# Cross-attention and FFN layer on one core: two of k's four feature chunks turned by DMA as fp16 parts, c turned scaled and split

## The reference

```
q = softmax over each head's 64 features of (Wq @ layernorm(x)), 8 heads, times 64**-0.5
k = softmax over the 1024 tokens of (Wk @ c);   v = Wv @ c
context = k v^T per head;  out = Wo @ (context^T q) + bo
x = x + out / |out| * g * sqrt(128)                      # norm over the 128 channels
x = x + layernorm(x) @ dequantised 4-bit weight + bias   # FFN, 1024 x 1024
```

## Time and profile before

| | us |
|---|---|
| median of 3 runs | 719.55 (717.13 to 721.21) |
| profiled execution | 717.66 |
| its span | 715.8 |
| PE busy | 655.5 (92%) |
| DVE busy | 547.5 (76%) |
| POOL busy | 482.8 (67%) |
| ACT busy | 448.4 (63%) |

### The profile page before, as it was taken

How to read it: one execution, slowest core, us unless ns; L and a number is a source line. 1 busy time by engine, 2 the same in 40 slices (tenths; PEclk the granted TensorE clock), 3 DMA queues, 4 the chain that set the end, 5 groups by cost and what they waited for, 6 DMA issues and landing times.

```text
span 715.8 us, 11150 instructions
## 1 busy us (share of the span) xinstructions
PE 655.5 (92%) x3320; PEld 419.8 (59%) x3320; DVE 547.5 (76%) x890; ACT 448.4 (63%) x743; POOL 482.8 (67%) x413
## 2 busy tenths in 40 slices
PE   4878699999999999999999999999999999999655
PEld 3645466666665666666665666666565666666232
DVE  3996897887888887887888887887888887886421
ACT  3666758566675848576775748576775748575411
POOL 3156484968768594958778594958778594957541
PEclk9979999999999999999999999999999999999977
DMA  8135135573735445463625445463726444453602
GB/s 294 60 59 134 43 79 130 100 164 89 163 59 161 89 111 129 98 161 88 172 48 164 85 114 128 95 161 88 175 45 170 79 109 79 91 104 88 119 29 59
DMA packets 180983, 78.95 MB, mean 110 GB/s; under 512 B 170440, under 2 KB 172000, under 8 KB 180960
## 3 DMA queue, kind: packets, MB, share of 16 engines
q1 hardware_dynamic: 174624, 55.61, 37.1%
q10 hardware_dynamic: 6336, 23.07, 9.5%
HBM read 28.32 MB, written 8.39 MB: 51 GB/s over the span
## 4 chain that ended last, share of the span: by engine, by line
PE 35%; POOL 25%; issue 19%; DVE 12%; ACT 6%; DMA 2%; SPq 1%; POOLq 0%; ACTq 0%; DVEq 0%
PE ps_m L1093 7%; POOL q_tok_lo L409 6%; PE ps_m L1032 3%; POOL x L474 3%; POOL q_exp L399 3%; POOL y L415 3%; DVE q_sum L773 3%; POOL c_lo L439 3%; PE ps_k L962 3%; POOL rn L458 2%; PE ps_k L964 2%; PE ps_k L963 2%; ACT k_exp L522 2%; DVE q_nmax L761 2%; PE ps_o L962 2%
## 5 line engine op out<-in xcount | busy, mean ns | idle before, releaser
L409 POOL TENSOR_TENSOR q_tok_lo<-q_exp,q_tok_hi 128x1024 f16<-128x1024 f32 x64 | 139.3, 2176 | 87.3 <-ACT q_tok_hi L538 87.3
L399 POOL TENSOR_TENSOR q_exp<-q_exp,q_rec 128x1024 f32<-128x1024 f32 x64 | 122.1, 1908 | 5.0
L1032 PE MATMUL ps_m<-k_t,c_t 128*128 128x512 f32 x256 | 120.0, 603 | 0.0
L527 ACT ACTIVATE q_exp<-q_exp 128x512 f32<-128x512 f32 x128 | 80.6, 630 | 44.3 <-DVE q_exp L766 44.2
L754 DVE TENSOR_REDUCE k_nmax<-ps_k 128x1 f32<-128x1024 f32 x64 | 78.1, 1220 | 39.4 <-PE ps_k L964 39.3
L522 ACT ACTIVATE k_exp<-ps_k,k_nmax 128x1024 f32<-128x1024 f32 x64 | 71.1, 1110 | 53.8 <-DVE k_nmax L754 53.8
L538 ACT ACTIVATE q_tok_hi<-q_exp 128x1024 f16<-128x1024 f32 x64 | 67.7, 1057 | 51.4 <-POOL q_exp L399 51.4
L761 DVE TENSOR_REDUCE q_nmax<-ps_q 128x8 f32<-128x512 f32 x128 | 87.3, 682 | 11.2 <-PE ps_q L964 9.6
L766 DVE TENSOR_TENSOR q_exp<-ps_q,q_nmax 128x512 f32<-128x512 f32 x128 | 88.5, 692 | 5.1 <-POOL q_tok_lo L409 0.2
L962 PE MATMUL ps_q<-wq_hi,xn_lo 128*128 128x512 f32 x128 | 74.8, 585 | 7.1 <-DVE q_exp L766 5.7
L773 DVE TENSOR_REDUCE q_sum<-q_exp 128x16 f32<-128x1024 f32 x64 | 77.4, 1209 | 0.7 <-ACT q_exp L527 0.7
(11 more groups left out here) (150 smaller groups left out, 1420.1 us busy)
## 6 DMA issues: line engine op xcount, KB each, us to landing
x_res<-in_x ACTq DMA_DIRECT2D x16, 512.0 KB, 3.3
out_x<-y SPq DMA_DIRECT2D x15, 512.0 KB, 2.9
x_in<-in_x ACTq DMA_DIRECT2D x14, 512.0 KB, 4.8
c_in<-in_ctx ACTq DMA_DIRECT2D x14, 512.0 KB, 6.1
x_in<-in_x SPq DMA_DIRECT2D x2, 512.0 KB, 6.3
c_in<-in_ctx SPq DMA_DIRECT2D x2, 512.0 KB, 7.6
q_hi<-q_tok_hi SPq DMA_TRANSPOSE x64, 3.1
q_lo<-q_tok_lo SPq DMA_TRANSPOSE x64, 3.1
```

The source lines that it names most:

```text
L399: nc.gpsimd.tensor_tensor(pair, pair, rec.unsqueeze(2).to_broadcast([P, 2 * HEADS, DH]), ALU.mult).then_inc(qs_done, 1)
L409: nc.gpsimd.tensor_tensor(q_tok_lo[p % 2][:], q_exp[:, 2 * p:2 * p + 2, :].rearrange("p t d -> p (t d)"), q_tok_hi[p % 2][:], ALU.subtract ...
L527: nc.scalar.activation(q_exp[:, j, :], q_exp[:, j, :], ACT.Exp).then_inc(qexp_done, 1)
L1032: last = nc.tensor.matmul(ps_m[:], c_t[s][:, t, :], k_t[:, t, :], start=(t == 0), stop=(t == TC - 1))
```

## The change

Chunks 0 and 1 of k (`TURNED = 2`) are no longer turned by PE. Their exponentials are raised by 2^12 (`k_bias`, one small ACT instruction each), ACT rounds them to fp16 (`high_k`), POOL makes the rest (`low_k`), and SP turns both parts by DMA (`turn_k`, four a batch). Chunks 2 and 3 are turned as before, now in steps 3 and 4. For each block of tokens `mix_m` makes three fp16 products of 256 columns for chunks 0 and 1, and one fp32 product of 256 columns for chunks 2 and 3. c is scaled by `c_fit` while it is moved: twice by ACT (fp16 `c_t_hi`, fp32 `c_t`), and DVE makes the fp16 rest `c_t_lo`. `c_unit` and `c_fit` are made at step 6; the factor from `vo` is made once; `undo_g` is two instructions a batch where `fit_g` was five. `exp_k` of chunks 2 and 3 waits for `low_k` of chunks 0 and 1, whose buffers it overwrites. To make room, `x2n_hi` and `x2n_lo` lie in `spare`, and `x2_hi` and `x2_lo` in `zero_bc`.

```diff
+C_RANGE = 2.0 ** 12
+K_LIFT = float(np.log(2.0 ** 12))
+TURNED = 2
...
+c_t_hi = [sb(f"c_t_hi{s}", [P, TC, P], F16) for s in range(2)]
+c_t_lo = [sb(f"c_t_lo{s}", [P, TC, P], F16) for s in range(2)]
...
+k_t_hi = sb("k_t_hi", [P, TC, TURNED * P], F16)
+k_t_lo = sb("k_t_lo", [P, TC, TURNED * P], F16)
+k_t = sb("k_t", [P, TC, HID - TURNED * P])
...
+    def turn_k(b, j):
+        for tok, turned, done, turned_sem in ((k_hi, k_t_hi, khi_done, khi_turned),
+                                              (k_lo, k_t_lo, klo_done, klo_turned)):
+            sp.wait_ge(done, TURNED * b + j + 1)
+            if b > 0:
+                sp.wait_ge(m_ready, b)
+            sp.dma_start_transpose(turned[:, :, j * P:(j + 1) * P], tok[j][:]).then_inc(turned_sem, 16)
...
             turn_q(c, 3, "lo")
         if do_a:
+            for j in range(TURNED):
+                turn_k(a, j)
             for p in range(2):
                 turn_q(a, p, "hi")
                 turn_q(a, p, "lo")
...
+        def low_k(j):
+            pool.wait_ge(khi_done, TURNED * a + j + 1)
...
+            nc.gpsimd.tensor_tensor(k_lo[j][:], k_exp[:, j, :], k_hi[j][:], ALU.subtract).then_inc(klo_done, 1)
...
             if j == 0 and do_c:
                 scale_q(c, 3)
+            if j == 0 and do_a:
+                low_k(0)
             if j == 0 and do_c:
                 low_q(c, 3)
+            if j == 1 and do_a:
+                low_k(1)
...
+            if j < TURNED:
...
+                nc.scalar.activation(k_bias[:, j:j + 1], k_nmax[:, j:j + 1], ACT.Identity,
+                                     bias=k_lift[:]).then_inc(kbias_done, 1)
+                act.wait_ge(kbias_done, TURNED * b + j + 1)
...
+                bias = k_bias[:, j:j + 1]
+            else:
+                act.wait_ge(klo_done, TURNED * b + j - 1)
+                bias = k_nmax[:, j:j + 1]
+            nc.scalar.activation(k_exp[:, j % 2, :], ps_k[:], ACT.Exp, bias=bias,
                                  accum_out=k_sum[:, sums, j:j + 1]).then_inc(kexp_done, 1)
+        def high_k(j):
+            act.wait_ge(kexp_done, 4 * a + j + 1)
...
+            nc.scalar.activation(k_hi[j][:], k_exp[:, j, :], ACT.Copy).then_inc(khi_done, 1)
...
+        def move_tc(b, sb_, h):
+            turned = (ps_ta, ps_tb)[h][:].rearrange("p (t c) -> p t c", t=4)
+            act.wait_ge(tc_ready, 2 * b + h + 1)
+            act.wait_ge(cfit_steps, 2 * (b + 1))
...
+            nc.scalar.activation(c_t_hi[sb_][:, 4 * h:4 * h + 4, :], turned, ACT.Identity,
+                                 scale=c_fit[:]).then_inc(cthi_done, 1)
+            nc.scalar.activation(c_t[sb_][:, 4 * h:4 * h + 4, :], turned, ACT.Identity,
+                                 scale=c_fit[:]).then_inc(tc_moved, 1)
...
+            if j == 0 and do_a:
+                move_tc(a, s, 1)
+                high_k(0)
...
-            if 1 <= j < 5 and do_a:
-                move_tk(2 * (j - 1))
-            if j in (1, 2) and do_a:
-                move_tk(2 * (j - 1) + 1)
-            if do_a:
-                exp_q(j)
-            if j == 0 and do_f:
                 act.wait_ge(x2n_done, f + 1)
...
-                nc.scalar.activation(x2n_hi[:], og[:], ACT.Copy).then_inc(x2hi_done, 1)
+                nc.scalar.activation(x2n_hi, og[:], ACT.Copy).then_inc(x2hi_done, 1)
+            if j == 0 and do_a:
+                exp_k(a, s, 1)
+                exp_q(0)
+                high_k(1)
             if j == 0 and do_c:
                 high_q(c, 3)
+            if j == 1 and do_a:
+                exp_k(a, s, 2)
+                exp_q(1)
...
-            if j == 2 and do_f:
+            if j == 2 and do_a:
+                exp_q(2)
+            if j == 3 and do_a:
+                move_tk(0)
+                exp_k(a, s, 3)
+                move_tk(1)
...
-            if j in (6, 7) and do_n:
-                move_tc(j - 6)
-            if j == 7 and do_n:
-                exp_k(n, 1 - s, 0)
+            if j >= 5 and do_a:
+                exp_q(j)
             if j == 6 and do_n:
+                move_tc(n, 1 - s, 0)
...
+            if j == 7 and do_n:
+                exp_k(n, 1 - s, 0)
...
+        def fit_c():
...
+            nc.vector.tensor_scalar(c_unit[:], c_top[:], UNIT_FLOOR, 1.0 / C_RANGE, ALU.max,
+                                    ALU.mult).then_inc(cfit_steps, 1)
+            dve.wait_ge(cfit_steps, 2 * n + 1)
+            nc.vector.reciprocal(c_fit[:], c_unit[:]).then_inc(cfit_steps, 1)
+        def low_tc(b, sb_, h):
+            dve.wait_ge(tc_moved, 2 * b + h + 1)
+            nc.vector.scalar_tensor_tensor(out=c_t_lo[sb_][:, 4 * h:4 * h + 4, :].rearrange("p t c -> p (t c)"),
+                                           in0=(ps_ta, ps_tb)[h][:], scalar=c_fit[:],
+                                           in1=c_t_hi[sb_][:, 4 * h:4 * h + 4, :].rearrange("p t c -> p (t c)"),
+                                           op0=ALU.mult, op1=ALU.subtract).then_inc(ctlo_done, 1)
...
-            if do_a:
+            if do_a and j > 0:
...
             if j < 3 and do_a:
-                if j == 2:
-                    sum_q(a, 0)
                 max_k(a, j + 1)
-            if j == 0 and do_f:
+            if j == 0 and do_a:
+                shift_q(0)
+                low_tc(a, s, 1)
+            if j == 2 and do_a:
+                sum_q(a, 0)
+            if j == 1 and do_f:
                 dve.wait_ge(x2hi_done, f + 1)
...
-                nc.vector.tensor_tensor(x2n_lo[:], og[:], x2n_hi[:], ALU.subtract).then_inc(x2lo_done, 1)
+                nc.vector.tensor_tensor(x2n_lo, og[:], x2n_hi, ALU.subtract).then_inc(x2lo_done, 1)
...
             if j == 7 and do_n:
+                low_tc(n, 1 - s, 0)
                 max_k(n, 0)
...
-                last = nc.tensor.matmul(ps_m[:], c_t[s][:, t, :], k_t[:, t, :], start=(t == 0),
+                three(ps_m[:, 0:TURNED * P], c_t_hi[s][:, t, :], c_t_lo[s][:, t, :], k_t_hi[:, t, :],
+                      k_t_lo[:, t, :], start=(t == 0), stop=False)
+                last = nc.tensor.matmul(ps_m[:, TURNED * P:], c_t[s][:, t, :], k_t[:, t, :], start=False,
                                         stop=(t == TC - 1))
             if t1 == TC:
...
-            if 1 <= j < 5 and do_a:
-                transpose_k(2 * (j - 1))
+            if j in (3, 4) and do_a:
+                transpose_k(2 * (j - 3))
+            if j == 1 and do_c:
+                mix_out(0)
             if do_a:
                 project_q(j)
-            if 1 <= j < 5 and do_a:
-                transpose_k(2 * (j - 1) + 1)
-            if j == 0 and do_a:
-                project_k(a, 1, (0,))
+            if j in (3, 4) and do_a:
+                transpose_k(2 * (j - 3) + 1)
             if j == 0 and do_c:
                 mix_g()
-            if j == 0 and do_a:
-                project_k(a, 1, (1,))
-            if j == 1 and do_c:
-                mix_out(0)
             if j in (2, 3) and do_f:
-                if j == 2:
+                if j == 3:
                     spread_rs()
                 feed_forward(0, (j - 2,))
-            if 1 <= j < 3 and do_a:
+            if j < 3 and do_a:
                 project_k(a, j + 1)
...
-            if j == 7 and do_n:
-                transpose_c(1)
             if j == 7 and do_a:
                 mix_m(4, 5)
             if j == 7 and do_n:
                 project_k(n, 0)
             if j == 7 and do_a:
                 mix_m(5, TC)
+            if j == 7 and do_n:
+                transpose_c(1)
```

More of the change, by code:

```diff
@@ L125, in build @@
         k_rec = sb("k_rec", [P, HC])
-        k_t = sb("k_t", [P, TC, HID])
+        k_lift = sb("k_lift", [P, 1])
+        k_bias = sb("k_bias", [P, TURNED])
+        k_hi = [sb(f"k_hi{j}", [P, N], F16) for j in range(TURNED)]
+        k_lo = [sb(f"k_lo{j}", [P, N], F16) for j in range(TURNED)]
+        k_t_hi = sb("k_t_hi", [P, TC, TURNED * P], F16)
+        k_t_lo = sb("k_t_lo", [P, TC, TURNED * P], F16)
+        k_t = sb("k_t", [P, TC, HID - TURNED * P])
         q_tok_hi = [sb(f"q_tok_hi{r}", [P, 2 * HID], F16) for r in range(2)]
@@ L153, in build @@
         ffn_rows = sb("ffn_rows", [P, OUT], BF16)
-        x2n_hi = sb("x2n_hi", [P, N], F16)
-        x2n_lo = sb("x2n_lo", [P, N], F16)
-        x2_hi = sb("x2_hi", [P, TC, P], F16)
-        x2_lo = sb("x2_lo", [P, TC, P], F16)
+        x2n_hi, x2n_lo = (spare[:].bitcast(F16)[:, h * N:(h + 1) * N] for h in range(2))
+        x2_hi, x2_lo = (zero_bc[:].bitcast(F16)[:, h * N:(h + 1) * N].rearrange("p (t c) -> p t c", t=TC)
+                        for h in range(2))
         y = sb("y", [P, OUT])
@@ L635, in iteration @@
                         nc.scalar.activation(rs_t[:], ps_o[1][:, 0:P], ACT.Copy).then_inc(rs_moved, 1)
[L636 to L639 removed]
                     if j == 3 and do_a:
+                        exp_q(3)
                         high_q(a, 0)
```

106 lines of the change are left out of this document (67 added, 39 removed).

## The result

The changed kernel takes 737.5 us (735.1 to 740.6, median of 4 runs); the kernel before, on the same chip, 720.4. The ratio is 1.0245, with a 95% interval of 1.0215 to 1.0276: slower by 17 us, where I had forecast 9. The profiled execution has a span of 735.6 us; before, 715.8. That of the kernel before is 2.7 us faster than its median, so what the profiles differ by adds up to 20 and not to 17.

What follows compares the result with a forecast made beforehand. The bound was a closed ring of POOL waits of 40.16 us, not PE; the ring grows to 41.0. 717.66 + 12 - 2 = 728 for the profiled execution, 728 to 730 for the median, forecast 729; range 703 to 739.

Steps and rivals of the forecast that it cites:

- POOL's closed ring bounds the pass, PE doesn't: Whole pass: POOL's waits close a ring of 40.16 us; PE's saving counts only as far as this shortens.
- the ring: Closed waits: POOL from first `q_tok_lo` through additions 20.45, to `nmr2` 3.15, to next first `q_tok_lo` 16.56 us.
- N: The end of `nmr2`, from which the prediction counts times in a pass, in us.
- PE's products and transposes: PE: dropped transposes and cheaper `mix_m` products save 2.7 us a pass (0.1 to 2.7), leaving 36.7.
- `x2n_lo` falls into `q_tok_lo`: DVE ready at N + 7.1 waits for POOL until N + 8.65; first `q_tok_lo` at N + 17.4, pass 41.0 us.
- 14 x 0.85 = 12: Iterations 2 to 15, having all three stages: each 0.85 us longer, 12 us in all.
- the collision: DVE's two-SBUF-input `x2n_lo` stands still until POOL's `q_tok_lo` ends, a wait of 1.5 us; chance 0.48.
- The rival without a collision: `x2n_lo` goes ahead of POOL's `q_tok_lo`: 39.6 to 39.1 us a pass, 704 to 708 in all; chance 0.26.
- Iterations 0, 1 and last: -2: Iterations 0 and 1, without FFN or collision, and the last `mix_m`: 2 us of PE's saving credited.
- The clock falls: Rival: PE idle ahead of `mix_out(0)` drops the clock to 1.2 GHz each pass, 36 us on top, 765; chance 0.06.

Runs made afterwards that it cites:

- e3: Kernel before, with four of the eight fp32 products of each `mix_m` left out: 717.4 us.
- e1: Changed kernel, with `x2n_lo` on DVE replaced from the second batch on by a one-input maximum over the same 128x1024 elements: 727.5 us.
- e8: Kernel before, with the first `q_tok_hi` of a pass moved up on ACT, right behind the fourth exponential of k: 737.2 us.
- e6a: Changed kernel, with `x2n_lo` moved up on DVE behind `shift_q(0)` and POOL's first `k_lo` held back until it is done: 726.8 us.
- e9: Changed kernel with `x2n_lo`, `sum_q(0)` and first `q_tok_hi` earlier, POOL waits and `shift_q(0)` first at the start, and `rs_t` ahead of that `q_tok_hi` on ACT: 702.1 us.
- e5: Changed kernel, with two POOL waits in iterations 0 and 1 that hold `low_k(1)` and `low_q(c, 3)` behind DVE's set-up instructions: 731.6 us.
- e4: Changed kernel, with DVE's order of before in iterations 0 and 1 alone (`shift_q(0)` ahead of `g_hi` and `max_k(1)`): 731.0 us.
- e45: Changed kernel with both the edits of e4 and e5: 729.0 us.
- e10: Changed kernel, with PE's order of before at the head of iteration 1: first half of k's second product ahead of `mix_g`: 735.2 us.
- e2: Kernel before, with one more POOL instruction (x2 less x2, unread) in each FFN iteration, between `scale_q(c, 3)` and `low_q(c, 3)`: 720.2 us.
- e11: Kernel of e9 with e10's edit to PE's order at the head of iteration 1: 699.4 us.

## Why the prediction came out as it did

- *POOL's closed ring bounds the pass, PE doesn't*: right that PE's saving gains nothing alone (e3), and that a link of the ring counts (e1). But I had put PE too far behind: in e8 the stretch behind N is 1.6 shorter and the pass is not. And from N to the first `q_tok_lo` the ring itself runs through PE (e6a).
- *PE's products and transposes*: the prices of the products are right (0.11, 0.76 for four). PE's busy time fell by 1.4 in the pass and not by 2.7; in e9, where PE hardly waits, it is 37.05 in 39.04 us. I can't say how much of the difference is waiting too short for a bracket.
- *`x2n_lo` falls into `q_tok_lo`*: right in place (N + 7.15, forecast 7.1), in length (2.80) and in effect (N + 17.35, a pass of 40.7 to 41.1). The term 14 x 0.85 = 12 measured 2.89 + 8.8 - 0.6 = 11.1, and 1.6 of that is a fall of the clock in iteration 2 (below). e1 and e6a show the mechanism: without the collision a pass is 0.64 to 0.78 shorter.
- *The rival without a collision*: I gave it 39.1 to 39.6 a pass. It is 40.1 to 40.3, as before the change. I had let `sum_q(0)` come as soon as DVE was free, but the chain N, `k_exp`, PE, `k_nmax`, `k_exp`, PE stands in front of it. Without the collision the change would have gained nothing.
- *"Iterations 0, 1 and last: -2"*: **the step that failed.** It measured +9.2 in iterations 0 and 1, and -0.5 behind the last `m_t`. I had said that without an FFN there is no collision, and looked for `x2n_lo` alone. But the set-up has DVE instructions of 128x1024 in both iterations, the change puts two `k_lo` a batch beside them, and it puts `shift_q(0)` behind an instruction that waits. The collisions are shown (e5: 5.7 of the 9.2 us at the second `m_t`). The order's part is not separated from them (e4, e45), e10 adds 0.75, and some 3 us of the start stay open. The saving that I had credited to PE came only at the end.
- *The clock falls*: I gave it 0.06 as a thing of each pass. It was not a thing of each pass: in the steady passes the granted clock is 1.00. The lower level came in the start (0.83 in iteration 1, 0.92 before) and once more, below.

With the start right the forecast would have been 729 + 2 + 9 = 740.

## What to carry to other kernels

Where every pass is a ring of waits, take the time from the ring, check it by leaving work out on the busiest engine, and ask how far behind that engine stands. Once one link is shortened the next is found by the bracket behind it: here it took three edits (the collision, `sum_q(0)`, `rs_t`) until PE's saving was worth 1.3 us a pass, and the first two alone gave nothing over the kernel before. The saving is needed for it: the kernel before has PE busy for 39.39 in a pass, more than the 38.84 of e9. The orders of e9 in the kernel before I did not run. And lay every new POOL instruction against all DVE instructions it can meet, those of the set-up too, and not only in the steady pass.

## What the runs showed of the hardware

- VectorE and GpSimd don't meet through semaphores alone. A collision costs both sides: the DVE instruction waits for POOL's that was first, and POOL's next waits for DVE's (`k_lo` 3.12, `q_tok_lo` 3.06 in e2). DVE instructions with one SBUF input were held up as well where they are TENSOR_SCALAR (0.68 to 2.63, 0.74 to 1.81), while a TENSOR_REDUCE was not (1.21 in e1). The Trainium skill, "SBUF — State Buffer", section "Who interferes with whom", says both: `tensor_scalar` can enter a mode with two ports, `tensor_reduce` on trn2 can't, and issue order decides who blocks. The trace agrees in each of these cases. Not every TENSOR_SCALAR is held up: `xn` (128x1024, at 353.20) takes 0.81 beside POOL's `rn` (128x8, 353.13 for 1.65), and it takes 0.75 to 0.82 in all runs. Had I applied the first of these to the set-up, I would have looked for the collision there.
- The clock can differ behind equal idle times. In iteration 2 PE was idle for 0.70 and then 1.26 us ahead of the FFN's second eight products, in the changed kernel and in e4:
```profile
131.16 3.45 PE L1203 MATMUL ps_m<-w_int,zero_bc 128*128 128x512 f16 x8 [1.26 <-DMA zero_bc<-spare]
```
```profile
130.53:134.87 4.34, 3.71 (x10) 1.47 (x11) 1.61 (x4) 3.13 (x7) 2.61 (x3) 0.61 1.19 184
```
```profile
124.71 1.90 PE L1205 MATMUL ps_m<-w_int,zero_bc 128*128 128x512 f16 x8 [1.26 <-DMA zero_bc<-spare]
```
The middle one is the window around the first (PE busy 3.71, granted clock 0.61 as a mean over both levels): its products ran at the level of 1.2 GHz, e4's at 2.4. It cost 1.6 us once, over half of iteration 2's excess of 2.89. The trace of e1 has the same fall (3.45), that of e10 has the same 1.26 without it (1.90), and its iteration 2 is 1.70 shorter. In the start the level differs between e9 and e11, whose code is the same up to there.
